# Layer 3 of a four-layer model: opening and soft mixture run as one software pipeline over eight sequences

## What is computed

```
xn = layernorm(x)
s  = attention(xn);  g = silu(ffn(xn))
x  = x + s * g
```

```
xn       = layernorm(x, gamma, beta)              # a second layernorm, of the first one's output
logits   = (xn / |xn| * scale) @ (mu / |mu|)      # 512 tokens x 256 slots, per sequence
dispatch = softmax of logits over the tokens
combine  = softmax of logits over the slots of a token
slot_in  = dispatch.T @ xn                        # 256 slots x 128
h        = gelu(slot_in @ w1[e] + b1[e])          # expert e on its own 16 slots, hidden 32
slot_out = h @ w2[e] + b2[e]
out      = combine @ slot_out                     # back to 512 tokens x 128
```

## Time and profile before

| | us |
|---|---|
| median of 3 runs | 3489.22 |
| lowest, highest | 3480.53, 3489.5 |
| the profiled execution, its own time | 3490.4 |
| its span, first to last instruction | 3488.7 |
| PE busy in the span | 3189.1 (91%) |
| DVE, ACT, POOL busy | 2552.8, 1702.3, 826.1 |

### The profile page before, as it was taken

The page is one execution under the profiler, slowest core; times in us unless marked ns, Lnnn a source line. Parts: engine busy times, 40 slices in busy tenths (PEclk is TensorE's granted clock), DMA queues, the critical chain, the costliest instruction groups (busy, mean ns, idle before and its releaser), DMA issues. The chain is left out here.

```text
span 3488.7 us, 58230 instructions
## 1 busy us (share of the span) xinstructions
PE 3189.1 (91%) x20742; PEld 2493.5 (71%) x20742; DVE 2552.8 (73%) x5471; ACT 1702.3 (49%) x3928; POOL 826.1 (24%) x665
## 2 busy tenths in 40 slices
PE   5999998888888799998577999999999999999998
PEld 4777674545445577786456888888888888888887
DVE  4878776775858545455443788888888888888888
ACT  2545542121212244433343566666666666666666
POOL 2111001010000200000100334444444444444443
PEclk9999998989989889989677999999999999999999
DMA  2001101000000000001100000000000010000000
GB/s 51 2 4 49 49 1 46 1 0 1 1 1 1 1 1 1 1 1 35 39 0 1 9 15 20 21 21 21 21 21 11 19 21 14 20 21 21 21 1 25
DMA packets 43461, 52.99 MB, mean 15 GB/s; under 512 B 8678, under 2 KB 27177, under 8 KB 43177
## 3 DMA queue, kind: packets, MB, share of 16 engines
q1 hardware_dynamic: 36082, 45.32, 5.2%
q10 hardware_dynamic: 7094, 3.94, 0.5%
HBM read 38.50 MB, written 10.75 MB: 14 GB/s over the span
## 5 line engine op out<-in xcount | busy, mean ns | idle before, releaser
L70 PE MATMUL banks<-scratch 128*128 128x128 f32 (+3 forms) x3584 | 699.8, 324 | 2.6 <-ACT scratch L2865 2.6
L70 PE MATMUL banks<-nT,w 128*128 128x512 f32 x1184 | 587.5, 615 | 53.6 <-DVE hidden L1594 35.5
L70 PEld LDWEIGHTS banks<-scratch 128*128 128x128 f32 x3584 | 471.4, 192 | 64.9 <-issue 60.3
L70 PEld LDWEIGHTS banks<-scratch,tb 128*128 128x128 f32 x2560 | 357.0, 192 | 102.2 <-issue 61.7
L70 PE MATMUL banks<-scratch,tb 128*128 128x128 f32 x2560 | 369.0, 275 | 0.0
L2930 POOL TENSOR_TENSOR scratch<-scratch,aT 128x1024 f32<-128x1024 f32 x128 | 359.1, 2806 | 4.5 <-DVE aT L2752 4.5
L70 PEld LDWEIGHTS banks<-nT,w 128*128 128x128 f32 x1184 | 205.3, 196 | 214.5 <-issue 146.8
L78 DVE SCALAR_TENSOR_TENSOR scratch<-scratch,tb 128x512 f32<-128x512 f32 (+3 forms) x512 | 340.1, 706 | 8.4
L78 DVE SCALAR_TENSOR_TENSOR scratch<-tb,nn,banks 128x512 f32<-128x512 f32 (+3 forms) x512 | 267.8, 544 | 76.7 <-PE banks L70 72.5
L2752 DVE TENSOR_TENSOR aT<-banks,turn 64x1024 f32<-64x1024 f32 x256 | 312.9, 1222 | 5.7
L2922 POOL TENSOR_TENSOR scratch<-backwards,nn 128x512 f32<-128x512 f32 x128 | 133.3, 1042 | 773.5 <-ACT nn L2842 773.5
(11 more groups left out here) (394 smaller groups left out, 5512.6 us busy)
## 6 DMA issues: line engine op xcount, KB each, us to landing
tb<-head_rows SPq DMA_DIRECT2D x32, 512.0 KB, 7.2
turn<-head_turns SPq DMA_DIRECT2D x64, 128.0 KB, 2.7
head_turns<-loads SPq DMA_DIRECT2D x16, 256.0 KB, 2.9
head_turns<-rotation SPq DMA_DIRECT2D x16, 256.0 KB, 3.0
xs<-in_x SPq DMA_DIRECT2D x8, 256.0 KB
w<-in_L_Wqk SPq DMA_DIRECT2D x16, 128.0 KB, 2.1
out<-xs SPq DMA_DIRECT2D x8, 256.0 KB, 2.3
w<-in_L_w1T SPq DMA_DIRECT2D x1, 1280.0 KB, 9.4
```

The costliest lines, as they stand in the source:

```text
L70: return self.T.matmul(out, lhsT, rhs, start=start, stop=stop, skip_group_check=True)
```

## The change

Layer 3's opening and its mixture become one pipeline over all 8 sequences, with one barrier at its end in place of eight. Each engine has one program with 13 slots (`m3_slots`); in slot s it does each of its steps for the sequence s, s-1, s-2 and so on, and buffers exist twice (`lanes_m`, `m3_rows`). PSUM banks have a count of fillings and one of emptyings each. The waits stay with semaphores, each a constant.

What else changes:

- The second layernorm's moments go: POOL works out the second factor from the first (`second_power`: two products, a sum and a power on 128x4).
- Gamma goes into DVE's scaling, beta from DVE to POOL (`beta`, 128x512).
- The column lengths of mu go from Sqrt on ACT and a reciprocal on DVE to one power on POOL over 128x256 (in `unit_power` for sequence 0, with which `unit_rows` of sequence 0 on DVE waits for `m3_length`).
- The four products with the token sums (L83, 128x256 each) go; the output is divided instead (`divide`, 128x512).
- 16 and 16 small expert matmuls become 4 and 4 of 128 columns over 4 experts at once; a mask on POOL (`own_expert`, 128x512) keeps each slot's own expert. b1 goes into Gelu's bias, and the two transposes of the slots' outputs go.
- Gelu is 4 activations of 128x128. Exp and Gelu or Tanh now alternate once per slot instead of once per chunk.
- All parameter loads go on SP's queue, mu first, Wv and Wo behind the small ones and ahead of the heads' loads; each has its own semaphore, and no barrier waits for them. The products of Wv and Wo stand at the end of PE's program.

The core of the diff:

```diff
     def layer3(self):
         k = self
-        for c in range(CHUNKS):
-            k.open_layer(c, k.nT3[:, B * c:B * c + B, :], 0)
-            if c == 0:
-                k.layer3_products()
-            k.soft_mixture(c)
-            k.meet()
+        k.m3_pe()
+        k.m3_dve()
+        k.m3_act()
+        k.m3_pool()
+        k.meet()
```

PE's program (the helpers hold the matmuls; `take(bank)` waits until the bank is empty):

```diff
+        directions()
+        for s in k.m3_slots():
+            if 0 <= s - 1 < SEQS:
+                dispatch_turn(s - 1)
+            if 0 <= s - 2 < SEQS:
+                outputs(s - 2)
+            if 0 <= s - 1 < SEQS:
+                slots(s - 1)
+            if 0 <= s - 1 < SEQS:
+                opened_rows(s - 1)
+            if 0 <= s < SEQS:
+                units(s)
+            if 0 <= s - 1 < SEQS:
+                hidden(s - 1)
+            if 0 <= s - 1 < SEQS:
+                combine_turn(s - 1)
+            if 0 <= s < SEQS:
+                slot_logits(s)
+            if 0 <= s < SEQS:
+                token_logits(s)
+            if 0 <= s - 1 < SEQS:
+                slot_out(s - 1)
+        T.wait_ge(k.m3_products.sem, 32)
```

Three of the new steps in full:

```diff
+        def second_power(b):
...
+            small(G.tensor_tensor(r2, r["r"], r["r"], ALU.mult))
+            G.wait_ge(k.pool.sem, k.pool.n)
+            small(G.tensor_tensor(r2, r2, v, ALU.mult))
+            G.wait_ge(k.pool.sem, k.pool.n)
+            small(k.ts(r2, r2, 1e-5, None, ALU.add, eng=G))
+            G.wait_ge(k.pool.sem, k.pool.n)
+            small(G.tensor_tensor(r2, r2, k.minus_half[:, 0:TPB], ALU.pow), k.m3_rr)
...
+        def unit_power(b):
+            r = k.m3_rows[b % 2]
+            done()
+            if b == 0:
+                m = k.mu_scratch[:, 1, :]
+                k.m3_emptied_of(G, 7, "directions")
+                small(G.tensor_tensor(m, m, k.minus_half[:, 0:1].broadcast_to([P, 256]), ALU.pow), k.m3_length)
...
+        def dispatch(b):
+            t, r = k.lanes_m[b % 2], k.m3_rows[b % 2]
+            A.wait_ge(k.m3_ms.sem, b + 1)
+            k.m3_filled_by(A, 4, "dispatch_turn", b - 2)
             for h in range(2):
...
+                m = A.activation(t["dspT"][:, h, :], k.bank(4 + h), ACT.Exp, bias=r["ms"][:, h:h + 1],
+                                 accum_out=r["ssum"][:, h:h + 1])
+            m.then_inc(*k.m3_emptied[4].up())
```

More of the change, by code:

```diff
@@ L34, in up, with again @@
         return self.sem, by
+    def again(self):
+        self.base, self.n = self.base + self.n, 0
+        return self
 def view(ap, dims, offset=0):
@@ L2281, in layer3_prepare @@
+        k.own, k.mu_scratch = k.sb("own", [P, 2, P]), k.sb("mu_scratch", [P, 2, 256])
         both = k.acc.rearrange("p (two h) t d -> p two (h t) d", two=2)
         k.wv3, k.wo3 = both[:, 0, :, :], both[:, 1, :, :]
[L2283 to L2296, removed]
@@ L2297, in layer3_prepare @@
-        k.m3_o, k.m3_ob, k.m3_oT, k.m3_so, k.m3_out = (
-            Count(nc, n) for n in ("m3_o", "m3_ob", "m3_oT", "m3_so", "m3_out"))
+        k.m3_mom, k.m3_r, k.m3_norm, k.m3_gt = (n.again() for n in (k.moments, k.rstds, k.scaled, k.gated))
+        k.m3_rr, k.m3_xg, k.m3_xb = (Count(nc, n) for n in ("m3_rr", "m3_xg", "m3_xb"))
+        k.m3_sq, k.m3_ss, k.m3_ru, k.m3_xu, k.m3_mx, k.m3_ms = (
+            Count(nc, n) for n in ("m3_sq", "m3_ss", "m3_ru", "m3_xu", "m3_mx", "m3_ms"))
+        k.m3_ds, k.m3_hm, k.m3_th = (Count(nc, n) for n in ("m3_ds", "m3_hm", "m3_th"))
@@ L2330, in layer3_prepare @@
             k.load_tables(q)
[L2332 to L2356, removed]
     def spread(self, h, first, n, at):
@@ L2602, in soft_mixture, with m3_slots, m3_filled_by, m3_emptied_of @@
-    def soft_mixture(self, c):
-        k = self
-        k.m3_norms = k.moments.n
-        k.m3_dve(c)
-        k.m3_pool(c)
-        k.m3_act(c)
-        k.m3_pe(c)
+    def m3_slots(self):
+        return range(0, SEQS + 5)
+    def m3_filled_by(self, eng, bank, *whose):
+        if whose in self.m3_turn:
+            eng.wait_ge(self.m3_filled[bank].sem, self.m3_turn[whose])
+    def m3_emptied_of(self, eng, bank, *whose):
+        if whose in self.m3_turn:
+            eng.wait_ge(self.m3_emptied[bank].sem, self.m3_turn[whose])
@@ L2621, in after @@
         if units > 0:
-            eng.wait_ge(count.sem, units)
+            eng.wait_ge(count.sem, count.base + units)
     def piece(self, eng, count, kind, piece, units):
```

582 lines of the change are left out of this document (370 added, 212 removed).

## The result

The changed kernel takes 3396.01 us (median of 4 runs, 3385.8 to 3404.62) where the kernel before, on the same chip, takes 3487.75 (median of 4 runs, 3480.53 to 3489.5). The ratio is 0.974, with a 95% interval of 0.9708 to 0.9772: 92 us less. The forecast said 3392. The profiled execution is the lowest of the four: 3385.8 us, its span 3384.4.

What follows compares the result with a forecast made beforehand. No engine bounds layer 3's 270.6 us stretch; steps hand over with little beside them. Fill 23 + power 27 + 7 x 15.0 + drain 18 = 173 us, giving 3392; its own range 3372 to 3412, with rivals 1 to 3 3361 to 3432.

Steps and rivals of the forecast that it cites:

- seven periods: The steady slots between first and last dispatch turn on PE: 15.0 us per sequence, with bounds 14.0 and 22.5.
- drain: Layer 3's end, from the last dispatch turn to the heads, with the Wv and Wo products: 18 us.
- the one it had followed: The wait loop per slot through token_max, unit_power, unit_rows, slot_logits, dispatch and slot_bias: 14.2 us at 2.4 GHz.
- fill, without the power: Layer 3's opening up to the first dispatch turn, leaving out the power of mu: 23 us with handovers.
- power of mu: POOL's power over 128x256 ahead of sequence 0's unit_rows, fully on the path: 27 us, half of 0.2 per column.
- input loads on the path: Waits for layer 3's parameter loads, taken as nothing, with 0 and 8 us as ends.
- ACT's table loads in the periods: Exp and Gelu switches, 2.6 us of ACT's slot, costed at nothing because ACT waits for PE and DVE anyway.
- rival 2: POOL's power of mu goes by the column and costs 52 to 66.6 us: 3417 to 3432 us; chance 0.10.
- I take 0.88: PE's granted clock in the steady slots, taken from layers 1 and 2; it makes the loop 14.8 us.
- rival 3: ACT's table switches are in the slot's loop: period 17 us and not 15, 3406 us; chance 0.08.
- rival 4: PE stays at 1.2 GHz in the slots: period 22.5 us, 3452 us; chance 0.04.
- The rival on the other side: Slower than before: the power ahead of sequence 0's unit_rows costs 135 us, 0.53 per column, or more; chance 0.02.

Runs made afterwards that it cites:

- e3_no_switch: The changed kernel with Gelu and the gate's Tanh replaced by Identity, so ACT's tables are not switched there; 3391.48 us in one run.
- e2_pow64: The changed kernel with only 64 of mu's 256 columns put through POOL's power; 3362.56 us in one run.
- e4_own_first: The changed kernel with own_expert ahead of beta and first_power in POOL's order; 3399.9 us in one run.
- e8_both: e1_sqrt with own_expert ahead of beta and first_power on POOL and total ahead of token_max on DVE; 3357.1 us in one run.
- e6_wait_loads: e1_sqrt with one barrier for all loads, the heads' first ones included, ahead of the stage's work; 3390.76 us in one run.
- e7_pack_only: The kernel before with only the packed expert matmuls, the mask on POOL and the bias inside Gelu; 3451.79 us, ratio 0.99.
- e1_sqrt: The changed kernel with POOL's power of mu replaced by Sqrt on ACT and a reciprocal on DVE; 3362.19 us, ratio 0.964 to the kernel before.

## Why the prediction was right, and where its terms were off

The time was right to 4 us (3392 and 3396), and so was the stage's mechanism: fill, a power on the path, seven periods set by a loop of waits, drain. That it was right to 4 us is luck: the power was 14.1 us over its term and the periods 8.8 under theirs. The power lies within the 12 to 47 us that the forecast allowed, if far from its 27; the period lies under its 14 to 16; and the loop that set the period was not the one it had followed. The stage came out 7.2 us over its sum. The heads were 1.6 us shorter, and the kernel before had a median 1.5 us lower than the one that the forecast started from, which leaves 4. Measured from PE's first dispatch turn (1696.02) to its last (1792.20) and to the heads (1811.74):

| term | forecast | measured |
|---|---|---|
| fill, without the power | 23 | 64.5 - 41.1 = 23.4 |
| power of mu | 27 | 41.1 |
| seven periods | 105 (7 x 15.0) | 96.2 (7 x 13.74) |
| drain | 18 | 19.5 |
| input loads on the path | 0 | 0 |
| ACT's table loads in the periods | 0 | 0 (e3_no_switch; its 0.6 is in the drain) |
| sum | 173 | 180.2 |

- **The power** is the first mis-sized term. The step was "I take half, 0.1 per column". The choice between the ends was a compromise between a product's row and a power's row, and e2_pow64 shows that there was nothing to compromise on: 0.159 us per column from 4 to 256 columns, 0.3 to 0.4 us per instruction. The earlier trace rows held a better guess. A product over 4 columns takes 0.24 to 0.31 there; subtracted from 1.04, this leaves 0.8 for 4 columns, 0.2 per column and 52 us, 10 over the measured 41.1 where 27 is 14 under it. I had written that number and halved it. Of rival 2 the mechanism, by the column, is what happens; its price, 52 to 66.6 us, is too high.
- **The period** is the second. The loop was summed to 13.75 us and measured 13.66 once POOL's order lets it bind (e4_own_first), and the true bound, 0.31 longer, ran through POOL's program order, which I had added up as work (7.7 us) but not followed as a line: beta and first_power stand ahead of own_expert. The largest error is the clock, 0.6 us per slot: "I take 0.88", and it was 1.00. I took it from stretches of other layers; PE's idle 2 us of a slot did not lower it. The nine handovers, 0.45, were counted on top of durations that overlap a little, and 0.2 was rounding. With the 0.1 by which the loop's sum was too high, that is 15.0 for a loop of 13.66. The mean of the seven, 13.74, is under the steady 13.97 because the first three distances and the last are shorter (13.07, 13.54, 13.90 and 13.65).
- **Fill and drain** hold within 0.4 and 1.5 us. The 1.5 is the drain's clock: the last outputs took 3.47 us in the changed kernel and 2.05 in e8_both.
- **The loads** cost nothing, as taken. DVE squares mu 4.8 us after its load was issued, with no idle time. e6_wait_loads shows 27.6 us for a wait for all of them.
- **Table loads**: rival 3 falls with e3_no_switch; "costed at nothing" was right for the periods, and so was its reason. There were 15 loads in the stage.
- **PE at 1.2 GHz** (rival 4) falls with the steady stretch at 1.00; e7_pack_only shows where it would have been true: the chunks keep 0.73.
- **The rival on the other side**, the power at over 135 us, was right in place and mechanism. At 41 us it is the largest item on the stage's path: taking it away gave another 38 us (e1_sqrt), a little more than packing gave.
- **The heads** moved by 1.6 us, within the 5 named.

## What to carry to other kernels

When a stage becomes a pipeline, follow each engine's program order as a line and not only its sum of work: the period here was set, by 0.3 us, by the place of a 1.26 us instruction on an engine that was busy 7.4 of 14 us, and each reordering uncovered the next loop a few tenths behind. A once-only instruction that becomes long is invisible in busy shares; ask of every new shape what it costs per column, with two sizes of the same operation. And compare stretches, not executions: here an untouched part moved by 12 us between two profiles, as much as several of the effects studied.

## What the runs showed of the hardware

- POOL's power costs 0.159 us per column of 128 partitions and 0.3 to 0.4 us besides, at 4, 64 and 256 columns; a two-input operation over 128x256 takes 0.73. DVE's reciprocal over 128x256 takes 1.75.
- PE's granted clock was 1.00 for 96 us of slots in which PE idled 2 us of every 14, while layer 2, with PE busy over 98% of 400 us, had 0.91 to 0.95. That last clock differed between the profiled executions with nothing changed there, and with it the start of layer 3, between 1631.5 us (clock 0.95) and 1647.9 (clock 0.91, e4_own_first).
- The last 20 us of the stage ran at 1.00, 0.92 or 0.85 in kernels with the same drain, which is 19.2, 20.7 to 20.9, or 22.2 us. What decides between them stays open.
- A table load on ACT took 1.28 us, and the activations stood 0.02 us before and 0.01 us behind it (changed kernel, 1757.52).
- Loads moved at 220 GB/s from SP's queue alone (e6_wait_loads) and at 229 with ACT's issuing too (the kernel before). The two sets of loads are not the same, so this bounds what the second queue brought only roughly: little.
